# One maximum over two PSUM banks: merging the key-logit maxima of a batch pair in a one-core decoder kernel

## What is computed

```python
def reference(x, ctx_4096, Wq, Wk, Wv, Wo, bo, g, w_gate, w_up, w_down):
    x = layernorm(x + attn(x))                 # softmax(q q^T) q at each of 512 positions, over the 32 batches
    x = layernorm(x + xattn(x, ctx_4096, ...)) # linear cross attention, 8 heads of 64
    x = layernorm(x + ffn(x, ...))             # gated MLP with group-quantized operands, 512 -> 1376 -> 512
    return x

def xattn(q, k, v, Wq, Wk, Wv, Wo, bo, g):
    qh = softmax(Wq q, axis=-2) * SCALE        # over the 64 rows of a head
    kh = softmax(Wk k, axis=-1)                # over the 512 positions   <- the change is here
    out = Wo (context(kh, Wv v) qh) + bo
    return out / norm(out) * g * sqrt(64)
```

## Time and profile before

| what | value |
|---|---|
| median of 3 runs | 730.14 us (729.62 to 1068.34) |
| span of the profiled execution | 729.4 us |
| PE busy | 665.2 us (91%) |
| DVE busy | 604.8 us (83%) |
| POOL busy | 507.2 us (70%) |
| ACT busy | 476.5 us (65%) |
| `k_max`, L939 | 82.2 us in 128 instructions |
| `exp_k`, L1704 | 87.4 us in 128 instructions |

### The profile page before, as it was taken

One profiled execution on the slowest core, in us unless ns is written; L12 is line 12 of the kernel. 1 busy time (PEld: TensorE's weight loads), 2 busy tenths in 40 slices (PEclk: granted clock), 3 DMA queues, 4 the chain that ended last, 5 costly groups with the idle time before them and its releaser, 6 DMA issues.

```text
span 729.4 us, 14548 instructions
## 1 busy us (share of the span) xinstructions
PE 665.2 (91%) x5520; PEld 367.1 (50%) x5520; DVE 604.8 (83%) x897; ACT 476.5 (65%) x869; POOL 507.2 (70%) x631
## 2 busy tenths in 40 slices
PE   0649898999999999999999999999999999899894
PEld 0648795344454454454554554444545554454451
DVE  2649867997978989998898988898977479999994
ACT  3329474887686787787787777767776544454543
POOL 1513645787888688778878887688777567845784
PEclk9957899999999999999999999999999999999998
DMA  9990011000100010010000000000000000001001
GB/s 310 163 245 4 24 38 59 15 15 1 30 2 28 3 31 18 13 30 1 31 30 1 31 29 2 30 24 3 27 1 1 2 1 1 30 36 39 30 30 72
DMA packets 21766, 26.95 MB, mean 37 GB/s; under 512 B 4033, under 2 KB 12225, under 8 KB 21697
## 3 DMA queue, kind: packets, MB, share of 16 engines
q1 hardware_dynamic: 21696, 26.02, 12.8%
HBM read 21.82 MB, written 4.19 MB: 36 GB/s over the span
## 4 chain that ended last, share of the span: by engine, by line
PE 70%; DVE 14%; issue 7%; POOL 5%; DMA 2%; ACT 2%; SPq 0%; POOLq 0%; DVEq 0%; ACTq 0%
PE banks L2501 9%; PE banks L2491 9%; PE banks L2538 8%; PE banks L2458 8%; PE banks L2468 8%; PE banks L2515 8%; PE banks L2443 4%; PE banks L2580 4%; PE banks L2426 3%; DVE big L854 3%; DMA big<-in_x_dram 2%; PE banks L2553 2%; PE banks L2545 2%; DVE big L859 2%; DVE big L1017 1%
## 5 line engine op out<-in xcount | busy, mean ns | idle before, releaser
L1637 ACT ACTIVATE big<-banks 128x512 f32<-128x512 f32 (+3 forms) x352 | 198.0, 592 | 96.6 <-PE banks L2491 45.5
L526 POOL TENSOR_TENSOR big<-big 128x512 f32<-128x512 f32 x128 | 134.8, 1066 | 10.3 <-DVE big L959 10.2
L1704 ACT ACTIVATE big<-banks,big 128x512 f32<-128x512 f32 x128 | 87.4, 687 | 21.8 <-DVE big L939 21.1
L518 POOL TENSOR_TENSOR big<-big 128x512 f32<-128x512 f32 x64 | 85.8, 1348 | 14.0 <-ACT big L1709 14.0
L939 DVE TENSOR_REDUCE big<-banks 128x1 f32<-128x512 f32 x128 | 82.2, 676 | 14.0 <-PE banks L2458 13.8
L945 DVE TENSOR_REDUCE big<-banks 128x16 f32<-128x1024 f32 x64 | 77.2, 1206 | 14.5 <-PE banks L2468 14.2
L2491 PEld LDWEIGHTS banks<-ident,big 128*128 128x128 f32 x512 | 55.3, 142 | 66.2 <-issue 43.4
L2501 PEld LDWEIGHTS banks<-ident,big 128*128 128x128 f32 x512 | 54.8, 141 | 63.9 <-ACT big L1637 36.9
L2491 PE MATMUL banks<-ident,big 128*128 128x128 f32 x512 | 81.4, 284 | 1.5 <-ACT big L1637 0.9
L950 DVE TENSOR_TENSOR big<-banks,big 128x1024 f32<-128x1024 f32 x64 | 77.8, 1215 | 4.0 <-PE banks L2501 2.7
L2501 PE MATMUL banks<-ident,big 128*128 128x128 f32 x512 | 77.6, 282 | 0.7 <-ACT big L1637 0.4
(11 more groups left out here) (108 smaller groups left out, 1219.3 us busy)
## 6 DMA issues: line engine op xcount, KB each, us to landing
big<-in_x_dram SPq DMA_DIRECT2D x8, 1024.0 KB, 13.6
big<-in_ctx_dram SPq DMA_DIRECT2D x16, 256.0 KB, 2.9
out_dram<-big SPq DMA_DIRECT2D x16, 256.0 KB, 2.0
big<-in_L_ffn_w_down_dram SPq DMA_DIRECT2D x4, 688.0 KB, 10.3
big<-in_L_ffn_w_gate_dram SPq DMA_DIRECT2D x10, 256.0 KB, 2.7
big<-in_L_ffn_w_up_dram SPq DMA_DIRECT2D x10, 256.0 KB, 2.9
wg_area<-in_L_xattn_Wq_dram SPq DMA_DIRECT2D x2, 128.0 KB, 11.4
wg_area<-in_L_xattn_Wk_dram SPq DMA_DIRECT2D x2, 128.0 KB, 6.9
```

Of the source, the lines that this page charges most:

```text
L518: pool.tensor_tensor(qfold[:, i % 2], e[:, :, :, 0:DH // 2], e[:, :, :, DH // 2:DH], ALU.add).then_inc(s.q_folded, 1)
L526: pool.tensor_tensor(e, e, r, ALU.mult).then_inc(s.p_ready, 1)
L1637: return act.activation(dst, src, ACT.Copy)
L1704: act.activation(EK[:, f % 2, par, i], bank[par], ACT.Exp, bias=kneg[:, par, i:i + 1], accum_out=ksum[:, f % 2, par, i:i + 1]).then_inc(s. ...
```

## The change

`k_max` loses its argument `par`. One instruction reduces banks 0 and 1 together (128 x 1024 in, 128 x 2 out) and writes both columns of `kneg`. It waits for both banks' logits. `k_max_ready` now counts one for each step, and both exponentials of a step wait for that one count. In DVE's list the merged instruction stands where the second one of the pair stood. Nothing changes in the lists of PE, ACT, POOL and SP but the number in this one wait.

```diff
-            def k_max(f, i, par):
-                dve.wait_ge(s.klog_ready, 8 * f + 2 * i + par + 1)
-                dve.tensor_reduce(kneg[:, par, i:i + 1], bank[par], X, ALU.max, negate=True).then_inc(s.k_max_ready, 1)
+            def k_max(f, i):
+                dve.wait_ge(s.klog_ready, 8 * f + 2 * i + 2)
+                dve.tensor_reduce(kneg[:, :, i], banks[:, 0:2], X, ALU.max, negate=True).then_inc(s.k_max_ready, 1)
...
-            k_max(2, 2, 0)
             scale_item(2)
             q_max(2, 1)
-            k_max(2, 2, 1)
+            k_max(2, 2)
...
-                k_max(f + 1, 3, 0)
-                k_max(f + 1, 3, 1)
+                k_max(f + 1, 3)
...
-            k_max(T - 3, 3, 0)
             clip_item(T - 4)
-            k_max(T - 3, 3, 1)
+            k_max(T - 3, 3)
...
-            k_max(T - 1, 3, 0)
             q_sum(T - 1, 1)
             scale_g(T - 2)
-            k_max(T - 1, 3, 1)
+            k_max(T - 1, 3)
...
-                act.wait_ge(s.k_max_ready, 8 * f + 2 * i + par + 1)
+                act.wait_ge(s.k_max_ready, 4 * f + i + 1)
```

More of the change, by code:

```diff
@@ L1088, in _ @@
             add_msg(1, 0)
-            k_max(0, 0, 0)
             transpose_probs(5)
-            k_max(0, 0, 1)
+            k_max(0, 0)
             add_msg(1, 1)
@@ L1100, in _ @@
             add_msg(3, 1)
-            k_max(0, 1, 0)
             transpose_probs(6)
-            k_max(0, 1, 1)
+            k_max(0, 1)
             add_msg(4, 0)
@@ L1112, in _ @@
             scale_aw(5)
-            k_max(0, 2, 0)
             clip_aw(3)
-            k_max(0, 2, 1)
+            k_max(0, 2)
             add_msg(6, 1)
@@ L1119, in _ @@
             x1_stats(0)
-            k_max(0, 3, 0)
-            k_max(0, 3, 1)
+            k_max(0, 3)
             scale_aw(6)
@@ L1125, in _ @@
             q_shift(0, 0)
-            k_max(1, 0, 0)
-            k_max(1, 0, 1)
+            k_max(1, 0)
             q_max(0, 1)
@@ L1134, in _ @@
             q_shift(0, 2)
-            k_max(1, 1, 0)
-            k_max(1, 1, 1)
+            k_max(1, 1)
             q_max(0, 3)
@@ L1143, in _ @@
             clip_aw(5)
-            k_max(1, 2, 0)
-            k_max(1, 2, 1)
+            k_max(1, 2)
             q_max(1, 1)
@@ L1148, in _ @@
             q_shift(1, 1)
-            k_max(1, 3, 0)
-            k_max(1, 3, 1)
+            k_max(1, 3)
             q_sum(0, 3)
@@ L1161, in _ @@
             q_sum(1, 0)
-            k_max(2, 1, 0)
-            k_max(2, 1, 1)
+            k_max(2, 1)
             x1_stats(3)
@@ L1177, in _ @@
             q_shift(2, 2)
-            k_max(2, 3, 0)
-            k_max(2, 3, 1)
+            k_max(2, 3)
             scale_item(3)
@@ L1193, in _ @@
             q_shift(3, 0)
-            k_max(3, 1, 0)
-            k_max(3, 1, 1)
+            k_max(3, 1)
             q_sum(2, 2)
@@ L1199, in _ @@
             q_sum(2, 3)
-            k_max(3, 2, 0)
-            k_max(3, 2, 1)
+            k_max(3, 2)
             q_max(3, 2)
@@ L1205, in _ @@
             clamp_ss(1)
-            k_max(3, 3, 0)
-            k_max(3, 3, 1)
+            k_max(3, 3)
             q_sum(3, 1)
@@ L1214, in _ @@
             scale_g(2)
-            k_max(4, 0, 0)
-            k_max(4, 0, 1)
+            k_max(4, 0)
             x1_stats(5)
@@ L1221, in _ @@
             q_sum(3, 2)
-            k_max(4, 1, 0)
-            k_max(4, 1, 1)
+            k_max(4, 1)
             quantize_x(0)
@@ L1227, in _ @@
             q_sum(3, 3)
-            k_max(4, 2, 0)
-            k_max(4, 2, 1)
+            k_max(4, 2)
             clamp_ss(2)
@@ L1236, in _ @@
             dequant_item(3)
-            k_max(4, 3, 0)
-            k_max(4, 3, 1)
+            k_max(4, 3)
             norm_y(2)
@@ L1244, in _ @@
             scale_item(5)
-            k_max(5, 0, 0)
-            k_max(5, 0, 1)
+            k_max(5, 0)
             x1_stats(6)
@@ L1251, in _ @@
             q_sum(4, 2)
-            k_max(5, 1, 0)
             x2_stats(2)
-            k_max(5, 1, 1)
+            k_max(5, 1)
             q_max(5, 1)
@@ L1257, in _ @@
             q_sum(4, 3)
-            k_max(5, 2, 0)
-            k_max(5, 2, 1)
+            k_max(5, 2)
             q_max(5, 2)
@@ L1265, in _ @@
             dequant_item(4)
-            k_max(5, 3, 0)
-            k_max(5, 3, 1)
+            k_max(5, 3)
             norm_y(3)
@@ L1273, in _ @@
             scale_item(6)
-            k_max(6, 0, 0)
-            k_max(6, 0, 1)
+            k_max(6, 0)
             quantize_x(1)
@@ L1282, in _ @@
             q_sum(5, 2)
-            k_max(6, 1, 0)
-            k_max(6, 1, 1)
+            k_max(6, 1)
             q_max(6, 1)
@@ L1287, in _ @@
             q_sum(5, 3)
-            k_max(6, 2, 0)
-            k_max(6, 2, 1)
+            k_max(6, 2)
             q_max(6, 2)
@@ L1295, in _ @@
             dequant_item(5)
-            k_max(6, 3, 0)
-            k_max(6, 3, 1)
+            k_max(6, 3)
             norm_y(4)
@@ L1336, in _ @@
             scale_x(7)
-            k_max(T - 5, 0, 0)
-            k_max(T - 5, 0, 1)
+            k_max(T - 5, 0)
             x1_stats(T - 4)
@@ L1343, in _ @@
             q_sum(T - 6, 2)
-            k_max(T - 5, 1, 0)
-            k_max(T - 5, 1, 1)
+            k_max(T - 5, 1)
             q_max(T - 5, 1)
@@ L1349, in _ @@
             q_sum(T - 6, 3)
-            k_max(T - 5, 2, 0)
-            k_max(T - 5, 2, 1)
+            k_max(T - 5, 2)
             q_max(T - 5, 2)
@@ L1357, in _ @@
             dequant_item(T - 6)
-            k_max(T - 5, 3, 0)
-            k_max(T - 5, 3, 1)
+            k_max(T - 5, 3)
             norm_y(9)
@@ L1367, in _ @@
             scale_x(8)
-            k_max(T - 4, 0, 0)
-            k_max(T - 4, 0, 1)
+            k_max(T - 4, 0)
             q_max(T - 4, 0)
@@ L1373, in _ @@
             q_sum(T - 5, 2)
-            k_max(T - 4, 1, 0)
-            k_max(T - 4, 1, 1)
+            k_max(T - 4, 1)
             x1_stats(T - 2)
@@ L1380, in _ @@
             q_sum(T - 5, 3)
-            k_max(T - 4, 2, 0)
-            k_max(T - 4, 2, 1)
+            k_max(T - 4, 2)
             q_max(T - 4, 2)
@@ L1389, in _ @@
             x1_stats(T - 1)
-            k_max(T - 4, 3, 0)
-            k_max(T - 4, 3, 1)
+            k_max(T - 4, 3)
             norm_y(T - 6)
@@ L1397, in _ @@
             scale_x(9)
-            k_max(T - 3, 0, 0)
-            k_max(T - 3, 0, 1)
+            k_max(T - 3, 0)
             scale_item(T - 3)
@@ L1402, in _ @@
             q_shift(T - 3, 0)
-            k_max(T - 3, 1, 0)
-            k_max(T - 3, 1, 1)
+            k_max(T - 3, 1)
             x2_stats(T - 6)
@@ L1407, in _ @@
             q_sum(T - 4, 2)
-            k_max(T - 3, 2, 0)
-            k_max(T - 3, 2, 1)
+            k_max(T - 3, 2)
             q_shift(T - 3, 1)
@@ L1438, in _ @@
             x2_stats(T - 5)
-            k_max(T - 2, 2, 0)
-            k_max(T - 2, 2, 1)
+            k_max(T - 2, 2)
             q_max(T - 2, 2)
@@ L1447, in _ @@
             q_max(T - 2, 3)
-            k_max(T - 2, 3, 0)
-            k_max(T - 2, 3, 1)
+            k_max(T - 2, 3)
             q_shift(T - 2, 3)
@@ L1455, in _ @@
             scale_g(T - 3)
-            k_max(T - 1, 0, 0)
-            k_max(T - 1, 0, 1)
+            k_max(T - 1, 0)
             q_sum(T - 2, 2)
@@ L1462, in _ @@
             q_shift(T - 1, 0)
-            k_max(T - 1, 1, 0)
-            k_max(T - 1, 1, 1)
+            k_max(T - 1, 1)
             x2_stats(T - 4)
```

24 lines of the change are left out of this document (8 added, 16 removed).

## The result

| | kernel before | changed kernel |
|---|---|---|
| median, first comparison | 730.71 us (4 runs) | 740.02 us (4 runs) |
| ratio, 95% interval | | 1.0116 [1.0091, 1.0141] |
| second comparison, beside three of the experiments | 730.54 us | 738.66 us |
| ratio, 95% interval | | 1.0109 [1.0090, 1.0128] |
| span of the profiled execution | 729.4 us | 735.9 us |

Forecast were 736.9 us, in a range of 728.5 to 743.0. The change costs about 1.1%, 8 to 8.5 us, which lies in the range; forecast were 6.8.

The account below looks back on a forecast made before the run. PE was taken to bound the cross attention except its start up to about 150 us. Losses through ACT's queue summed to 6.8 us, added to the 730.14 us median for 736.9 us, range 728.5 to 743.

Parts of the forecast that it names:

- merged maximum, added wait: At each key step: one merged maximum takes 1.22 us, saving 0.06; waiting for the second bank's logits counts as nothing.
- loop, tiles 7 to 10: Step 3 of these four loop tiles: the later exponential delays ACT's copies, 0.23 us on PE each, 0.9 together.
- (1, 3), with DVE's start gains: Where the chain passes from DVE through ACT to PE: 0.54 us later, 0.24 earlier by pairs saved ahead; 0.3 lost.
- (2, 2): Step with two other instructions between the maxima: two key copies behind the exponential slip by 2.5 us; PE loses 1.3.
- (4, 3) and (12, 3): Steps where PE needs the context copy behind the first exponential: all 0.55 us lands on PE, 1.1 for both.
- (13, 3): Step where the exponential slips from 489.51 to 490.39; the copy behind it has 0.1 us margin: 0.8 us lost.
- (15, 3): Last step, query sum and scaling of G between the maxima: exponential 2.28 us later, weight copy delayed, 2.0 on PE.
- the three small ones: Steps (2, 0), (12, 0) and (14, 2): margins of 0.3 to 0.7 us just used up, estimated 0.4 us together.
- The signs: Changed kernel's profile: 64 maxima of 1.2 us, DVE 4 us less, longer exponential waits, PE waits at five places.
- ACT swallows it: Rival: ACT, 65% busy, absorbs the delays, as PE's margins are often over 1 us; 729.8 us, chance 0.15.
- DVE's relief wins: Rival: DVE sets PE's schedule, so its saved 3.8 us and more come back; 726 us, chance 0.08.
- The loop tips over: Rival: ACT's gaps close and each of the loop's 28 steps pays 0.55 us on PE; 751 us, chance 0.09.

Follow-up runs that it names:

- the last step alone taken back: Changed kernel, but with the two separate maxima of before in the last step, (15, 3), alone; 735.31 us, ratio 1.0074.
- the altered order: ACT's list with copies ahead of the exponential at four places and the loop's norm of x2 behind two copies; 730.51 us with the merge, 728.61 without.
- the fastest one among them: Kernel before, 128 separate maxima, ACT's copies ahead of the exponential at four places, the loop's norm of x2 behind two copies; 728.61 us, ratio 0.9976.
- the one merged between neighbours: Changed kernel, merged only in the 52 steps where the pair stands together, two maxima in the twelve split steps; 732.98 us, ratio 1.0036.
- that with the 4.60 us wait: Kernel before with three extra copies to 8-bit floats on ACT (1280 + 2 x 768) ahead of the last step's exponential; ratio 1.0081.

## Why the prediction was right, and where its terms were off

The mechanism and the sign hold: a PE-bound kernel doesn't gain from freed DVE time, and loses through late exponentials in ACT's queue. The size was 6.8 us against 8 to 8.5. That it came so near is in part luck: the terms that the sum had came to 6.0 us in the trace instead of 6.8, with errors both ways, three that it didn't have added 3.1, and 0.3 came back at the end.

| step of the prediction | forecast | measured on PE |
|---|---|---|
| merged maximum, added wait | 1.22 us, nothing | 1.208 us, nothing |
| loop, tiles 7 to 10 | 4 x 0.23 = 0.9 | 4 x 0.26 = 1.04 |
| (1, 3), with DVE's start gains | 0.3 | 0.45 |
| (2, 2) | 1.3 | 1.46 |
| (4, 3) and (12, 3) | 0.55 + 0.55 | 0.53, and a net gain of 0.58 at tile 12 |
| (13, 3) | 0.8 | 0.35 |
| (15, 3) | 2.0 | 2.35 |
| the three small ones | 0.4 | 0.4 |
| clock at half behind (15, 3) | not seen | 1.41 |
| a wait for POOL, `sum_squares(13)` | not seen | 0.44 |
| clock at half near 644 us | not seen | 1.28, not to be ascribed |

*The missing term* is the clock. The prediction counted PE's waits as time lost once and took them all at full speed. The half clock near 558 us comes when the wait there is made long by other means (3.14 and 4.60 us) and stays away when the step is given its two maxima or ACT's order is changed.

*The signs* that the prediction named came: 64 maxima of 1.2 us, DVE 3.4 us less busy instead of 4, the exponentials' wait up by 17.7 us, and waits of PE for ACT's copies at all five places, the largest at the last. Only "in the loop a tile should take 0.2 us longer" holds for just the four tiles of the sum.

*(15, 3)* was 0.35 larger. "The merged one ends at 553.87 - 0.60 + 1.22" assumed that the work between moves ahead by the full 0.60. It didn't: DVE idled 0.39 us ahead of the scaling of G. The program has it wait for PE's product, which ended at 554.02, only 0.10 us before the reciprocal ahead of it, and 0.70 before it in the kernel before. The row names the reciprocal; that the late product is the reason is argued, not tested. DVE's timeline of the changed kernel:

```profile
553.98 0.14 DVE L963 RECIPROCAL big<-big 128x8 f32<-128x8 f32 x1
...
554.51 0.76 DVE L968 TENSOR_TENSOR big<-banks,big 128x256 f32<-128x256 f32 x2 [0.39 <-DVE big L963]
```

*(12, 3) and (13, 3)* were the terms of the sum that came out wrong. At (12, 3) the exponential is 0.54 us later than the work ahead of it, as forecast, and at (13, 3) it starts 0.84 later than before. But PE wasn't at the same point: delays add up only where the chain runs through the earlier one. Behind 453 us the kernel before had an accident of its own, which the changed one escaped. DVE and POOL at that point, before, then changed:

```profile
453.64 1.27 POOL L518 TENSOR_TENSOR big<-big 128x512 f32<-128x512 f32 x1 [0.57 <-ACT big L1709]
```

```profile
453.70 1.76 DVE L1010 TENSOR_TENSOR big<-big 128x512 bf16<-128x512 fp8e4 x1
```

```profile
454.56 0.69 DVE L1010 TENSOR_TENSOR big<-big 128x512 bf16<-128x512 fp8e4 x1
...
455.17 0.68 DVE L958 TENSOR_REDUCE big<-big 128x16 f32<-128x512 f32 x1
```

```profile
454.70 1.69 POOL L518 TENSOR_TENSOR big<-big 128x512 f32<-128x512 f32 x1 [0.57 <-ACT big L1657]
```

DVE's dequantization took 1.76 us when POOL's addition had started 0.06 us ahead of it, and 0.69 when it came first itself, while POOL then took 1.69 instead of 1.27. So the work behind it on DVE ran up to 1.07 us sooner relative to PE, and the 1.06 us that PE had lost by then shrank to 0.48 us behind (12, 3), its new delay included. At (13, 3) PE already stood 0.48 later and only the excess of 0.35 reached it. No run was made for this, but all fourteen traces agree: in the six where the dequantization comes second here (1.76 to 1.78 us; all have the separate maxima with their own waits) PE has no such gain, in the eight where it comes 0.13 to 0.15 us first PE gains 0.5 us at the same instruction.

*The wait for POOL at `sum_squares(13)`* is the same meeting with the opposite result. DVE and POOL of the changed kernel:

```profile
541.83 0.69 DVE L1010 TENSOR_TENSOR big<-big 128x512 bf16<-128x512 fp8e4 x1
```

```profile
541.86 1.56 POOL L539 TENSOR_TENSOR big<-big 128x512 f32<-128x512 f32 x1
```

POOL's operation takes 1.04 us in the kernel before and 1.56 here, where the dequantization starts 0.03 us ahead of it, and PE waits for it. With the last step alone taken back, whose lists are the same up to this point, POOL was 0.01 us ahead instead, took 1.04 us, and PE lost nothing here.

*The rivals.* "ACT swallows it" is right for most steps and wrong in the sum. "DVE's relief wins" fell: no version with the merge is below before. "The loop tips over" didn't come: the loss in the loop stayed at 0.26 us for each of four tiles.

The rule of the Trainium skill (Perfetto Trace Analysis, Optimizing Scalar/DVE Operations) that breaking up instructions may let work be completed sooner, where an unsaturated engine holds up others, agrees with these runs: the separate maxima are the faster ones, by 1.1% as the lists stand and by 0.26% with the altered order.

The half clock near 644 us can't be ascribed to the change. It starts there, between 637 and 650 us, in the changed kernel (in both of its profiles) and in nine of the eleven experiments with another kernel, the fastest one among them, and is missing in the kernel before, in the one merged between neighbours and in that with the 4.60 us wait. In each of the fourteen traces, these three included, PE waits 2.5 us for `dequant_hidden` at this point. Which executions get it stays open.

## What to carry to other kernels

Merging two instructions joins their results: the first consumer waits for both. Before doing it, look at what stands in the consumer's queue behind the first use, and at whether the engine that is relieved is the bound in that stretch at all. When a delay is followed on paper, measure each from the chain that it meets, not from the old clock time, and reckon that a wait of PE of about two microseconds can cost more than its length: behind those in this kernel's cross attention it was 1.3 to 1.5 us more. The cheap remedy was the order of the consumer's list: what the bound engine needs next goes ahead of what waits.

## What was not expected of the hardware

- TensorE's granted clock fell to half for 3.4 us around or right behind the end of waits of 1.67, 1.80, 2.09, 3.14 and 4.60 us in the cross attention, and stayed full behind waits of 0.18, 1.03 and, at (2, 2), 1.18 us in the changed kernel and 1.24 with its last step taken back. The 3.4 us at half cost 1.41 us, in the other traces 1.3 to 1.5. The wait's length alone doesn't tell: in the feed-forward stage the same wait of 2.5 us was followed by full clock in the kernel before and by half clock in the changed one, and waits of 1.54 and 1.69 us by full clock in both. The Trainium skill (Perfetto Trace Analysis, Matmul Optimizations) says that the matmul engine scales its power with its use, so that matmuls should run back to back. The granted clock behind these long waits agrees; the full clock behind the 2.5 us of the kernel before doesn't.
- The same DVE dequantization took 0.69 or 1.76 us depending on whether it started 0.14 us ahead of POOL's addition or 0.06 us behind it. Of the 420 in the fourteen traces, none of the 211 that started with no POOL operation of over 1 us under way took more than 0.71 us.
- A saturating copy to 8-bit floats on ACT had a table load of 1.28 us ahead of it and another ahead of the next exponential; copies to bf16 without saturation had none. Which of the two differences counts wasn't tried.
